# Six TensorE transposes per graph replaced by DMA transposes, five graphs in flight, and weight preparation interleaved with the first graphs

## The reference

```python
h = relu(layernorm(x)); x = x + gat(h, adj)            # 12 heads, scores + beta*adj, masked softmax
h = relu(layernorm(x)); x = x + directed(h, adj)       # 2 layers: exp(h W h^T / sqrt(384)) * adj, row-normalised,
                                                       #   times (h W_lin^T + b), layer norm (ddof=1), relu
h = relu(layernorm(x)); x = x + digcn(h, adj)          # 2 layers: softmax(h h^T / sqrt(384)) * adj, renormalised; upper,
                                                       #   diagonal and lower part meet three different products h W^T
h = relu(layernorm(x)); x = x + graphormer(h, adj)     # 12 heads, scores + adj, softmax, output product + bias
```

## Time and profile before

| | |
|---|---|
| median of 3 runs | 3015.51 us (3014.38 to 3015.76) |
| the profiled execution | 3016.85 us, its span 3015.1 us |
| PE busy | 2874.9 us, 95% of the span, 34304 matmuls |
| PE weight loads | 2231.5 us, 74% |
| DVE busy | 2493.4 us, 83% |
| ACT busy | 1769.2 us, 59% |
| POOL busy | 1397.1 us, 46% |
| DMA | 50.00 MB, mean 17 GB/s |
| mean granted TensorE clock | 0.99 |

### The profile page before, as it was taken

One profiled execution on the slowest core, in us unless ns is written; L12 is line 12 of the kernel. 1 busy time (PEld: TensorE's weight loads), 2 busy tenths in 40 slices (PEclk: granted clock), 3 DMA queues, 4 the chain that ended last, 5 costly groups with the idle time before them and its releaser, 6 DMA issues.

```text
span 3015.1 us, 88804 instructions
## 1 busy us (share of the span) xinstructions
PE 2874.9 (95%) x34304; PEld 2231.5 (74%) x34304; DVE 2493.4 (83%) x6895; ACT 1769.2 (59%) x6484; POOL 1397.1 (46%) x2313
## 2 busy tenths in 40 slices
PE   0699999999999999999999999999999999999996
PEld 0577777777777777777777777777777777777774
DVE  7478888888888888888888888888888888888874
ACT  3355665566566566566556656656656655665653
POOL 0145445444444544544544445454454454444443
PEclk9799999999999999999999999999999999999997
DMA  6000000000000000000000000000000000000000
GB/s 212 1 2 14 14 8 14 14 8 14 14 12 11 14 12 10 14 14 8 14 14 8 14 14 12 11 14 12 11 14 14 8 14 14 8 14 14 12 7 9
DMA packets 36091, 50.00 MB, mean 17 GB/s; under 512 B 3680, under 2 KB 35552, under 8 KB 35552
## 3 DMA queue, kind: packets, MB, share of 16 engines
q1 hardware_dynamic: 26464, 31.73, 3.4%
q10 hardware_dynamic: 9216, 12.59, 1.1%
HBM read 31.72 MB, written 12.58 MB: 15 GB/s over the span
## 4 chain that ended last, share of the span: by engine, by line
PE 92%; DVE 4%; POOL 1%; DMA 1%; ACT 1%; issue 1%; SPq 0%; POOLq 0%; DVEq 0%
PE bank L827 65%; PE bank L938 8%; PE bank L884 6%; PE bank L851 4%; PE bank L900 3%; PE bank L876 3%; PE bank L929 1%; PE bank L906 1%; PE bank L889 1%; DVE w_lo L647 1%; ACT t L563 1%; DMA t<-in_weights_dram 0%; DMA beta_col<-in_beta_dram 0%; DVE t L639 0%; DVE means L635 0%
## 5 line engine op out<-in xcount | busy, mean ns | idle before, releaser
L827 PE MATMUL bank<-w_hi,ht 128*128 128x384 f16 x3840 | 1032.9, 327 | 1.3 <-DVE t L707 1.3
L827 PE MATMUL bank<-ht,w_hi 128*128 128x128 f16 x9216 | 836.9, 220 | 12.1 <-DVE ht L685 8.2
L827 PE MATMUL bank<-ht,w_lo 128*128 128x128 f16 x4608 | 806.6, 220 | 0.0
L827 PEld LDWEIGHTS bank<-ht,w_hi 128*128 128x128 f16 x9216 | 721.0, 98 | 62.3 <-issue 29.2
L827 PE MATMUL bank<-w_lo,ht 128*128 128x384 f16 x1920 | 627.5, 327 | 0.0
L563 ACT ACTIVATE t<-t,few 128x128 f32<-128x128 f32 x1536 | 596.0, 398 | 0.7 <-DVE few L716 0.6
L827 PEld LDWEIGHTS bank<-w_hi,ht 128*128 128x128 f16 x3840 | 376.6, 98 | 231.3 <-issue 2.6
L449 POOL TENSOR_TENSOR v<-v,row 128x384 f32<-128x384 f32 x256 | 256.8, 1003 | 572.2 <-ACT v L530 572.2
L827 PEld LDWEIGHTS bank<-ht,w_lo 128*128 128x128 f16 x4608 | 454.0, 99 | 0.0
L554 ACT ACTIVATE qk<-bank 128x256 f16<-128x256 f32 x576 | 218.2, 379 | 301.4 <-PE bank L827 301.4
L544 ACT ACTIVATE ht<-bank 128x384 f16<-128x384 f32 x384 | 188.2, 490 | 320.4 <-PE bank L851 318.9
(11 more groups left out here) (108 smaller groups left out, 5384.1 us busy)
## 6 DMA issues: line engine op xcount, KB each, us to landing
x<-in_x_dram SPq DMA_DIRECT2D x64, 192.0 KB, 2.3
out_dram<-h ACTq DMA_DIRECT2D x64, 192.0 KB, 1.9
t<-in_weights_dram SPq DMA_DIRECT2D x19, 576.0 KB, 4.9
adj<-in_adj_dram SPq DMA_DIRECT2D x64, 64.0 KB, 2.2
row<-in_rows_dram SPq DMA_DIRECT2D x1, 3648.0 KB, 11.5
bias_qk<-in_qk_bias_dram SPq DMA_DIRECT2D x1, 3.0 KB, 11.2
beta_col<-in_beta_dram SPq DMA_DIRECT2D x1, 0.5 KB, 11.0
```

Of the source, the lines that this page charges most:

```text
L827: m = nc.tensor.matmul(out, a, b, start=(first and n == 0), stop=(last and n == 3 * len(left) - 1))
```

## The change

- `STREAMS` goes from 4 to 5, with a set of tiles and semaphores for the fifth. To make room `pt` goes: the turned probabilities lie in `t`, the partial sums of the Graphormer scores and the spread reciprocals in `qk`, and GAT's edge terms in a tile `edge`.
- `turn` leaves PE. ACT writes the high half of ReLU(h) into one half of a float16 row of `qk`, DVE the low half into the other, both from `h` in SBUF, and SP issues one DMA transpose of the 128x768 block into `ht`. PE waits on `turned_in` of the stream. SP now waits for the stream's `low` ahead of each transpose, and it issues 384 of them, all from its one queue.
- The weights are staged in places that hold late weights' halves afterwards (`w_hi` and `w_lo` of numbers 15 to 18) and in one spare tile. The preparation is cut into pieces that stand between the steps of the first graphs (`w` in the strings). The subtraction of the means goes from DVE to ACT. PE waits for single weights, and others for single rows, where they are first needed.
- The order is now a string for the opening, one for a round of five graphs repeated 10 times, and one for the closing.

```diff
-STREAMS = 4
+STREAMS = 5
...
-TURNS = {
-    "tensor": ("201231121320210030123032032203030101101321322010003003312302232031321101230103103310101212212032"
...
-LATE = {"tensor": [42, 30, 18], "vector": [48, 31, 16],
-        "scalar": [39, 31, 19], "pool": [17, 11, 4], "sync": [1, 0, 0]}
+OPENING = {
...
+    "sync":
+        "wwwww0ww1wwww0wwwww4w120www032w101032102143",
+}
+BODY = {
...
+REPEATS = 10
+CLOSING = {
...
+        HS = [q[:, 0].rearrange("p c a t -> p (c a t)") for q in QK]
...
+        PT = [t[:, 0] for t in T]
+        flat_qk = [q[:].rearrange("p w c a t -> p (w c a t)") for q in QK]
+        PARTS = [q.bitcast(F32).rearrange("p (h k) -> p h k", h=H) for q in flat_qk]
+        RT = [q[:, 2 * D:4 * D].bitcast(F32).rearrange("p (c k) -> p c k", c=C) for q in flat_qk]
...
+        def wait_turned(eng, r, s, layer):
+
+            eng.wait_ge(turned_in[s], 16 * (6 * r + layer + 1))
...
+                elif name == "turn":
+                    wait_for(sp, r, s, "low", step)
+                    sp.dma_start_transpose(HT[s][:].rearrange("p w c t -> p (w c) t"), HS[s]).then_inc(turned_in[s], 16)
...
                 elif name == "turn":
 
-                    wait_filled(act, r, s, step)
-                    nc.scalar.activation(HT[s][:, 0, :, i * P:(i + 1) * P],
-                                         bank_of(s, step)[:, 0:D].rearrange("p (c k) -> p c k", c=C),
-                                         ACT.Relu).then_inc(done[s]["turn_hi"], 1)
+                    wait_for_normed(act, r, s, layer, i)
+                    nc.scalar.activation(HS[s][:, 0:D], HN[s][:, i], ACT.Relu).then_inc(done[s]["high"], 1)
...
                 elif name == "turn":
-                    wait_for(v, r, s, "turn_hi", step)
-                    nc.vector.scalar_tensor_tensor(
-                        out=HT[s][:, 1, :, i * P:(i + 1) * P], in0=bank_of(s, step)[:, 0:D].rearrange("p (c k) -> p c k", c=C),
-                        scalar=0.0, in1=HT[s][:, 0, :, i * P:(i + 1) * P], op0=ALU.max,
-                        op1=ALU.subtract).then_inc(done[s]["turn_lo"], 1)
+                    wait_for(v, r, s, "high", step)
+                    nc.vector.scalar_tensor_tensor(out=HS[s][:, D:2 * D], in0=HN[s][:, i], scalar=0.0, in1=HS[s][:, 0:D],
+                                                   op0=ALU.max, op1=ALU.subtract).then_inc(done[s]["low"], 1)
...
-                elif name == "turn":
-                    if layer in (DIR_B, DIG_B):
-                        wait_for(pe, r, s, "biased", ("cnorm", layer - 1, i))
-                    else:
-                        wait_for(pe, r, s, "normed", ("norm", layer, i))
-                    for c in range(C):
-                        last = nc.tensor.transpose(bank_of(s, step)[:, c * P:(c + 1) * P], HN[s][:, i, c * P:(c + 1) * P],
-                                                   ident)
...
                 elif name == "proj":
 
-                    wait_for(pe, r, s, "turn_lo", ("turn", layer, G - 1))
+                    wait_turned(pe, r, s, layer)
+                    wait_weights(pe, r, W0[layer] + 1)
...
+            def set_up():
+                for w in range(N_W):
+                    wait_staged(act, w)
+                    if w in CENTRED_W:
+                        act.wait_ge(w_sums, 2 * CENTRED_W.index(w) + 2)
+                        for c in range(C):
+                            mean = means[:, 8 + CENTRED_W.index(w) * C + c:9 + CENTRED_W.index(w) * C + c]
+                            nc.scalar.activation(stage_of(w)[:, c], stage_of(w)[:, c], ACT.Identity,
+                                                 bias=mean).then_inc(w_centred, 1)
```

More of the change, by code:

```diff
@@ L125, in banks_of @@
 def banks_of(name):
-    return {"load": 1, "turn": 1, "proj": 1, "vals": 1, "scores": HPC, "flip": 1, "mix": 1, "back": 1, "project": 1,
+    return {"load": 1, "proj": 1, "vals": 1, "scores": HPC, "flip": 1, "mix": 1, "back": 1, "project": 1,
             "gram": 1, "aturn": 1, "context": 1, "scale": 1}.get(name, 0)
@@ L194, in has_part @@
                 or name == "aturn" and not directed)
[L195 to L201, removed]
+    return name in ("load", "turn")
+RELEASE = {"load": "evicted", "proj": "low", "vals": "evicted", "scores": "scored",
+           "flip": "evicted", "mix": "high", "scale": "evicted", "aturn": "evicted",
+           "back": "x_added", "project": "x_added", "gram": "gram"}
 def release_of(step, j):
@@ L218, in turns_of @@
     own = [x for x in steps if has_part(engine, x)]
[L219 to L222, removed]
-    assert not any(queues), engine
-    return turns
+    taken = [0] * STREAMS
+    for mark in OPENING[engine] + BODY[engine] * REPEATS + CLOSING[engine]:
+        if mark == "w":
+            yield None
+        else:
+            s = int(mark)
+            n, k = divmod(taken[s], len(own))
+            taken[s] += 1
+            yield s, n, own[k]
 class Plan:
@@ L864, in step_of @@
                     j, g = i // G, i % G
-                    wait_for(pe, r, s, "turn_lo", ("turn", layer, g))
-                    product(bank_of(s, step)[:, 0:D], [turned(s, c, slice(g * P, (g + 1) * P)) for c in range(C)],
+                    wait_turned(pe, r, s, layer)
+                    wait_weights(pe, r, W_V[layer][j])
+                    product(bank_of(r, s, step)[:, 0:D], [turned(s, c, slice(g * P, (g + 1) * P)) for c in range(C)],
                             [weight(W_V[layer][j], c) for c in range(C)]).then_inc(filled[s], 1)
                 elif name == "scores":
-                    wait_for(pe, r, s, "proj_lo", ("proj", layer, C - 1))
+                    wait_for(pe, r, s, "low", ("proj", layer, C - 1))
                     cols = slice(i * P, (i + 1) * P)
@@ L903, in step_of @@
                 elif name == "back":
-                    wait_for(pe, r, s, "mixed_hi", ("mix", layer, i))
+                    wait_for(pe, r, s, "high", ("mix", layer, i))
                     for c in range(C):
-                        last = nc.tensor.transpose(bank_of(s, step)[:, c * P:(c + 1) * P], OT[s][:, c], ident)
+                        last = nc.tensor.transpose(bank_of(r, s, step)[:, c * P:(c + 1) * P], OT[s][:, c], ident)
                     last.then_inc(filled[s], 1)
                 elif name == "project":
-                    wait_for(pe, r, s, "mixed", ("mix", layer, i), 1)
-                    product(bank_of(s, step)[:, 0:D], [(OH[s][0][:, c], OH[s][1][:, c]) for c in range(C)],
+                    wait_for(pe, r, s, "low", ("mix", layer, i))
+                    wait_weights(pe, r, W0[layer] + 3)
+                    product(bank_of(r, s, step)[:, 0:D], [(OH[s][0][:, c], OH[s][1][:, c]) for c in range(C)],
                             [weight(W0[layer] + 3, c) for c in range(C)]).then_inc(filled[s], 1)
@@ L932, in step_of @@
                     kinds = 1 if layer in (DIR_A, DIR_B) else 2
-                    wait_for(pe, r, s, "aturn" if layer in (DIR_A, DIR_B) else "masked", ("aturn", layer, None))
+                    wait_for(pe, r, s, "evicted" if layer in (DIR_A, DIR_B) else "masked", ("aturn", layer, None))
                     for j in range(kinds):
```

468 lines of the change are left out of this document (268 added, 200 removed).

## The result

The changed kernel takes **2870.05 us** (median of 4 runs, 2868.06 to 2871.32) where the kernel before takes 3015.64 beside it (4 runs, 3014.38 to 3015.92): a ratio of 0.9517, 95% interval 0.9501 to 0.9534. That is 4.8% less, inside the range and 18 us above the forecast of 2852. The span of the profiled execution is 2868.4 us.

The account below looks back on a forecast made before the run. PE was taken to bound the middle: 64 graphs at 42.5 us make 2720, plus 84 lost at the beginning and 48 at the end, 2852 us against 3015.1. The forecast's own range was 2812 to 2890, the wider one 2812 to 2940.

Parts of the forecast that it names:

- What bounds the middle, and PE's 2.0 us: Middle: PE has no gap, so removing six turns saves 2.0 us a graph, from 44.53 to 42.5.
- provided that PE still never waits: Middle: the condition on which a graph comes to 42.5 us and 64 graphs to 2720.
- How long a transpose takes: DMA transpose of 128 x 768 float16 into `ht`: 4 us taken, between bounds of 2.3 and 5.2.
- The upper bound: Transpose time from 768 packets at 62 ns over 16 engines, 3.0 us, plus 2.2 to land: 5.2 us.
- The allowance: Tightest place, `context` of layer 1 to `proj` of layer 2: a transpose up to 4.9 us costs PE nothing.
- The same count leaves the other layers more room: Layers other than the tightest place have more than 4.9 us for a transpose, so only that place pays, once a graph.
- The beginning, 84: Opening: first product at about 35 us plus 49 us of filling the streams, 84 us lost.
- The end, 48: Closing: 40 us as before, plus 8 for two or three exposed `turn`, each 3 us longer.
- Its base of 40: Closing of the kernel before: 31.6 us of PE idle plus 8 to 9 for the lower clock, 40 lost.
- Rival (a): Middle: transpose or its queue takes over 4.9 us; at 6.0, 1.1 more a graph, 2922; with (b) together 0.25.
- (b): Middle: DVE becomes the bound; a graph takes 43.5 us, total 2916, or 2980 without gain; with (a) together 0.25.
- (c): Slower than before: 128-byte pieces make transposes 8.2 us, PE stops 3.3 a graph, 3063; turning at 7.4; chance 0.09.

Follow-up runs that it names:

- pe_back: The changed kernel with three 128x128 float32 transposes of the identity put back on PE ahead of each layer's first product; 2987.12 us.
- no_transpose: The changed kernel without its 384 DMA transposes, ACT and DVE writing the halves straight into the tile that PE reads; 2870.18 us.
- pool_swap: The changed kernel with layer 4's two masks moved ahead of another stream's cnorm addition in POOL's repeated order; 2920.95 us.
- late_rest: The changed kernel with one waited-for 512-byte DMA ahead of the transposes of the five layers other than layer 2; 2968.07 us.
- double: The changed kernel with every DMA transpose made twice, first into a tile that nothing reads; 2931.29 us.
- late1w: The changed kernel with one 512-byte DMA, waited for on SP, ahead of each transpose; 3050.56 us.
- turn_only: The kernel before with the DMA transposes alone: four streams, old order with PE's turns struck out, old beginning; 3891.28 us.
- late2w: The changed kernel with two 512-byte DMAs, each waited for on SP, ahead of each transpose; 3862.23 us.
- late3: The changed kernel with three 512-byte DMAs, not waited for, issued on SP ahead of each transpose; 3102.49 us.

## Why the prediction was right, and where it was off

- **What bounds the middle, and PE's 2.0 us**: right. Without its waits a graph takes 42.82 - 0.34 = 42.48 us, 2.05 less than 44.53, where 2.0 was taken and the share had said 2.07; `pe_back` put 1.9 back.
- **"provided that PE still never waits"**: this is the step that failed. PE waits 0.34 us a graph, in two places that no term of mine held; 64 x 0.32 = 20 us is the whole miss in the middle. At most 0.07 of it are transposes (`no_transpose`). The larger part is POOL's order (`pool_swap`); the smaller part is DVE's by the trace. DVE was weighed by its busy share and its own waits, and POOL not at all: engines with idle time to spare still held PE up for a moment by the order of their work.
- **How long a transpose takes**: 4 us taken, 2.8 measured, inside the bounds. The upper bound took 62 ns a packet from the loads; the transposes' packets took (18.9% x 2868.4 - 3.4% x 3015.1) x 16 / 307344 = 23 ns. By the Trainium skill, Advanced Engine Details and Errata (X-Bar Transpose (TRN2)), transposing DMAs are as fast as ordinary ones: the trace agrees nearly, 2.8 against 2.3 us for the load of as many bytes. The estimate from the Trainium skill's VectorE: DVE Perf Modes (The three transpose paths), 7.9 us, is not what this kernel shows. The advice for TensorE that the prediction gives with it stands in that page's section Rules for kernel authors and is tied to a PSUM destination being fine; here, with PE the bound, PE time for the six turns costs 117 us (`pe_back`).
- **The allowance**: right place, 0.8 us too large (4.9 put, 4.1 measured). It decided nothing at 2.8 us. The error was to take POOL's row from a stretch near the end of the program, where no other stream's masks stood ahead of it. "The same count leaves the other layers more room" holds at 2.8 us; at 5.3 the five others together cost 0.87 us a graph (`late_rest`).
- **The beginning, 84**: the first product was put at 35 and came at 37.20, and the beginning lost 76: filling cost some 38 us behind it, not 49. **The end, 48**: it lost 52. Its base of 40 was too low, since the kernel before lost 49 there, and three slower `turn` were counted as 8 us, while doing away with the transposes gains nothing in all. The two together were put at 132, and 128 were lost, so part of that agreement is errors that cancel.
- **Rival (a)**: didn't happen, and its price was wrong: six transposes of 5.3 us cost 2.14 us a graph, not 0.4, of which the named place pays 1.21 and the others the rest, and 0.64 is paid at 4.05 us, below the allowance, where slow transposes come late. **(b)**: didn't happen; DVE is busy 187.73 of 212 us, 89% as counted, and PE waits for it 0.12 us a graph. **(c)** turned at a transpose of 7.4 us by my rule. It turns earlier: six transposes of 4.05 us (`double`) cost 61 us, of 5.3 us (`late1w`) 180, and on a line between them the 145.6 us of gain are used up at 4.9.

## What to carry to other kernels

In this kernel moving work from the bounding engine to DMA was worth that engine's own time per item, and next to nothing of the DMA's duration counted, since the order left it room; the same edit in an order without that room cost many times what it saves (876 us against 117). Count the allowance in the traffic of the middle, with what other streams put into the same in-order queues, and leave it for the slow transfer, not the median one. Both exchanges of two neighbours closed the gap that they aimed at and opened a larger one: look first for who stands behind the step that you delay. And an end of the program can't be read from one wait: the first transpose ended PE's longest wait there, yet doing away with it moved nothing, because the weights' preparation was the longer path.

## What the runs showed that I had not expected

- The price of a delay bends: 0.6, 2.1, 2.7 us a graph for 1.25, 2.5, 3.0 us, then 14.9 for 5.0.
- Three DMAs of 512 bytes ahead of a transpose of 192 KB on the same queue slow it from 2.8 to 4.5 us, while a whole transpose ahead of it slows it only to 2.9. The small ones make 144 packets each (509328 - 343428 packets in 1152 DMAs).
- Issuing a transpose holds SP for 1.21 us, a plain load for 0.33; now and then it takes up to 2.5 us (in `double`, with landing after 4.8).
- In the middle of `turn_only` and `late2w` PE was busy 795 and 811 of 1000 us, and the granted clock was 0.94 and 0.93, a mean between the two levels, 1.2 and 2.4 GHz; in `late3`, with 940 us busy, it was 1.00. The lower clock cost the two about 4 us a graph in PE's own work.
